# Experts' entry product: the last 64 features as three 64-row products on two row tiles

## The reference

```python
# layer 0: 8 experts of width 768, two of them weighted for each token
h_all = einsum('btc,che->bthe', x, w_fc)      # x: 520 tokens x 192 features
h = gelu(h_all of the token's experts)
o = sum over its experts of top_p * (h @ w_proj[expert])
# layer 1: 16 experts, eight of width 128 and eight of width 256, eight weighted for each token
for e in range(16):
    h = gelu(xt @ w1[:, off:off + wd])
    out = out + comb[:, e:e + 1] * (h @ w2[off:off + wd, :])
```

## Time and profile before

| what | value |
|---|---|
| median of 3 runs | 379.75 us (379.64 to 383.16) |
| the profiled execution's own time | 379.25 us |
| its span (first to last instruction of the program) | 377.4 us |
| granted clock of TensorE, mean | 0.857 |
| TensorE busy | 291.3 us of the span (77%) |
| VectorE busy | 268.6 us (71%) |
| ScalarE busy | 203.1 us (54%) |

### The profile page before, as it was taken

One profiled execution on the slowest core, in us unless ns is written; L12 is line 12 of the kernel. 1 busy time (PEld: TensorE's weight loads), 2 busy tenths in 40 slices (PEclk: granted clock), 3 DMA queues, 4 the chain that ended last, 5 costly groups with the idle time before them and its releaser, 6 DMA issues.

```text
span 377.4 us, 5949 instructions
## 1 busy us (share of the span) xinstructions
PE 291.3 (77%) x2232; PEld 266.6 (71%) x2232; DVE 268.6 (71%) x714; ACT 203.1 (54%) x486; POOL 23.6 (6%) x46
## 2 busy tenths in 40 slices
PE   5789979989999999999881042079631598999991
PEld 4577968889999999999771022058420588999991
DVE  1069173888888888798668997975368648888851
ACT  0034546677777777877271467570010667777750
POOL 8010000000000000000000005800000000000000
PEclk9999996999999999999996555569555579999997
DMA  7960400253153132000000000000500013543401
GB/s 235 261 267 1 148 0 4 85 176 125 50 177 116 61 146 72 29 1 2 0 3 0 0 1 2 0 0 2 195 0 1 0 24 114 162 160 126 113 0 43
DMA packets 11548, 27.36 MB, mean 72 GB/s; under 512 B 1496, under 2 KB 3144, under 8 KB 11520
## 3 DMA queue, kind: packets, MB, share of 16 engines
q1 hardware_dynamic: 10944, 26.03, 21.2%
q0 software_dynamic: 576, 0.96, 1.0%
HBM read 26.54 MB, written 0.45 MB: 72 GB/s over the span
## 4 chain that ended last, share of the span: by engine, by line
PE 62%; DVE 22%; ACT 7%; DMA 3%; issue 2%; SPq 2%; DVEq 0%; ACTq 0%
PE bank L585 26%; PE bank L647 9%; PE bank L569 7%; PE bank L632 4%; PE bank L630 4%; DMA embed_area<-w_tok_dram 3%; PE bank L847 2%; DVE embed_area L1510 1%; PE bank L552 1%; PE bank L832 1%; ACT hid_hi L982 1%; DVE bn L1187 1%; PE bank L844 1%; DVE stat_q L1395 1%; PE bank L857 1%
## 5 line engine op out<-in xcount | busy, mean ns | idle before, releaser
L585 PE MATMUL bank<-hid_hi,pj_parts 128*128 128x260 f32 x288 | 76.2, 286 | 1.7 <-DVE hid_lo L1282 1.7
L982 ACT ACTIVATE hid_hi<-hidden_area 128x260 fp32r<-128x260 f32 x144 | 55.9, 422 | 38.8 <-DVE hidden_area L1277 37.6
L1282 DVE TENSOR_TENSOR hid_lo<-hidden_area,hid_hi 128x260 fp32r<-128x260 f32 x144 | 56.6, 427 | 9.9 <-ACT hid_hi L982 0.3
L585 PEld LDWEIGHTS bank<-hid_hi,pj_parts 128*128 128x128 f32 x288 | 54.1, 188 | 2.5 <-DVE hid_lo L1282 2.0
L975 ACT ACTIVATE hidden_area<-bank 128x260 f32<-128x260 f32 x144 | 49.1, 377 | 6.9 <-PE bank L632 6.1
L585 PE MATMUL bank<-xt_hi,fc_hi 128*128 128x260 f32 x144 | 42.8, 297 | 1.3 <-ACT hidden_area L973 1.3
L632 PE MATMUL bank<-xt_lo,fc_lo 128*128 128x260 f32 x144 | 42.2, 293 | 0.0
L585 PE MATMUL bank<-xt_lo,fc_hi 128*128 128x260 f32 x144 | 41.5, 288 | 0.0
L630 PE MATMUL bank<-xt_lo,fc_hi 128*128 128x260 f32 x144 | 41.5, 288 | 0.0
L585 PE MATMUL bank<-xt_hi,fc_lo 128*128 128x260 f32 x144 | 41.3, 287 | 0.0
L647 PE MATMUL bank<-hid_hi,pj_parts 128*128 128x260 f32 x144 | 40.8, 283 | 0.0
(11 more groups left out here) (297 smaller groups left out, 559.3 us busy)
## 6 DMA issues: line engine op xcount, KB each, us to landing
raw_area<-fc_dram SPq DMA_DIRECT2D x8, 768.0 KB, 4.3
raw_area<-pj_dram SPq DMA_DIRECT2D x8, 576.0 KB, 5.4
xn<-comb_dram SPq DMA_DIRECT2D x12, 260.0 KB, 3.3
raw_area<-fc_dram SPq DMA_DIRECT2D x6, 512.0 KB, 4.0
hidden_area<-comb_dram SPq DMA_DIRECT2D x9, 260.0 KB, 3.3
raw_area<-pj_dram SPq DMA_DIRECT2D x6, 384.0 KB, 4.4
embed_area<-patches_dram SPq DMA_DIRECT2D x8, 256.0 KB, 4.7
embed_area<-w_tok_dram SPq DMA_DIRECT2D x8, 96.0 KB, 7.6
```

The source lines that it names most:

```text
L585: mm = pe.matmul(out, lhs[a], rhs[b], start=start and n == 0, stop=stop and n == 2, skip_group_check=True)
L982: act.activation(hid_hi[:, x % 3, tok], hid_w[:, x % 2, tok], ACT.Copy).then_inc(hid_hi_ready[y], 1)
L1282: dve.tensor_tensor(hid_lo[:, x % 3, tok], hid_w[:, x % 2, tok], hid_hi[:, x % 3, tok].bitcast(F32), ALU.subtract).then_inc(hid_lo_ready[y ...
```

## The change

The two 128-row matmuls with `x_mix` go. In their place come three products of 64 rows each (high x high, high x low, low x high), for the first half of the tokens on partitions 0 to 63 and for the second half on partitions 64 to 127, in turn. So `xt_hi[:, 1]` and `xt_lo[:, 1]` hold the first half's tokens on the lower and the second half's on the upper partitions, each made by two instructions of 64 x 260 in place of one of 64 x 520. The product low x low is no longer made. Per entry the array gets six matmuls of 64 rows where it had four of 128.

```diff
-        x_mix = xt_lo[:, 1, :]
...
                 pe.wait_ge(xhi_ready, 2 * n + (n + 1) // 2)
-                pe.wait_ge(xlo_ready, 2 * n)
+                pe.wait_ge(xlo_ready, 2 * n + (n + 1) // 2)
...
                             split3(out, (fc_hi[:, s, 0, cols], fc_lo[:, s, 0, cols]),
                                    (xt_hi[:, 0, tok], xt_lo[:, 0, tok]), True, False)
-
-                            pe.matmul(out, fc_hi[:, s, 1, cols], x_mix[:, tok], start=False, stop=False,
-                                      skip_group_check=True)
-                            mm = pe.matmul(out, fc_lo[:, s, 1, cols], x_mix[:, tok], start=False,
-                                           stop=True, skip_group_check=True)
-                        mm.then_inc(entry_mm[y], 1)
+                        if kind == "w":
+                            mm.then_inc(entry_mm[y], 1)
+                    if kind == "w":
+                        return
+                    for m, (f, v) in enumerate(((fc_hi, xt_hi), (fc_hi, xt_lo), (fc_lo, xt_hi))):
+                        for n in range(2):
+                            p, tok = slice(64 * n, 64 * n + 64), slice(n * HALF, (n + 1) * HALF)
+                            mm = pe.matmul(PB[PAIRS[k % 2][n]][:, 0:HALF], f[p, s, 1, cols], v[p, 1, tok], start=False,
+                                           stop=m == 2, skip_group_check=True)
+                            if m == 2:
+                                mm.then_inc(entry_mm[y], 1)
...
-                        k = DM // 2
-                        act.activation(xt_hi[k:DM, 1, :], xt[k:DM, 1, :], ACT.Copy).then_inc(xhi_ready, 1)
-                        act.activation(x_mix[0:k, :], xt[0:k, 1, :], ACT.Copy).then_inc(xhi_ready, 1)
+                        for n in range(2):
+                            q, tok = slice(64 * n, 64 * n + 64), slice(n * HALF, (n + 1) * HALF)
+                            act.activation(xt_hi[q, 1, tok], xt[q, 1, tok], ACT.Copy).then_inc(xhi_ready, 1)
```

More of the change, by code:

```diff
@@ L1220, in split_x @@
             def split_x(r):
[L1222 to L1225, removed]
+                every = slice(0, B * S)
+                parts = [(slice(0, chunk_rows(r)), 0, every)]
+                if r % 2:
+                    parts += [(slice(64 * n, 64 * n + 64), 1, slice(n * HALF, (n + 1) * HALF)) for n in range(2)]
+                else:
+                    parts += [(slice(0, DC), 1, every)]
+                for n, (p, j, tok) in enumerate(parts):
+                    dve.wait_ge(xhi_ready, 2 * (r - 1) + r // 2 + n + 1)
+                    dve.tensor_tensor(xt_lo[p, j, tok], xt[p, j, tok], xt_hi[p, j, tok].bitcast(F32),
                                       ALU.subtract).then_inc(xlo_ready, 1)
```

## The result

| | before | after |
|---|---|---|
| median | 379.69 us (4 runs) | **399.22 us** (4 runs, 397.2 to 406.94) |
| the profiled execution, its span | 379.25, 377.4 us | 400.2, 398.4 us |
| granted clock, mean | 0.857 | 0.842 |

The ratio is 1.051 (95% interval 1.045 to 1.056): slower by 5%, as forecast (396 us, 389 to 423). It leaves out the run of 406.94 us, a slow one, over 1.5% above the fastest of the same kernel.

What follows compares the result with a forecast made beforehand. PE alone was taken to bound the experts; 69 entries at + 0.266 us and three at + 0.38 made + 19.5 us, less 2.8 of waits, + 16.7 on 379.25: 396 us, range 389 to 423.

Steps and rivals of the forecast that it cites:

- What bounds the kernel: In both layers of experts PE alone bounds; what an entry takes more or less reaches the end 72 times.
- The pair, three slots for six: In each entry the six 64-row matmuls run side by side in three slots, 0.36 us; an entry gains 0.12 us.
- Rival 1: In the experts' entries the pairs don't overlap and take six slots in place of three: 422 us, chance 0.20.
- The change of tiling, 0.095 + 0.11 - 0.012: Before and behind an entry's pairs: stop plus unhidden weight load, less usual spacing; + 0.193 us each, + 0.386 an entry.
- Rivals 2 and 3: In the experts: a tiling change costs nothing, 371 us, chance 0.07; or the load stays hidden, 380 us, chance 0.09.
- Three entries at half clock, + 1.1 us: Entries 0 and 1 of layer 0 and 0 of layer 1 run at half clock, + 0.38 us each.
- The sum: Over the experts' entries: 69 at + 0.266 us and three at + 0.38 us, in all + 19.5 us before waits.
- The waits that hide a part, - 2.8 us: In the layers' first tiles PE's waits of 3.4 us for ACT and DVE shrink, hiding 2.8 us; bounds 0 and 3.4.
- What costs nothing: The split copies and subtraction on ACT and DVE, covered by the gate, and the later first-half result add no time.

Runs made afterwards that it cites:

- the run that has nothing else: The kernel before with only the last of an entry's ten matmuls using 64 rows in place of 128: 404.81 us, ratio 1.065.
- the repeat: The changed kernel run once more, unedited, for its spread and clock: 398.72 us, ratio 1.046.
- all in pairs: The changed kernel with all matmuls of the experts' entries and projections cut into pairs of 64 rows: 390.88 us, ratio 1.029.
- nine matmuls: The changed kernel with an entry's six 64-row matmuls replaced by three of 128 rows: 374.66 us; the kernel before without an entry's last matmul: 375.91 us.
- all in pairs, sooner: Same instructions as all in pairs, reordered on TensorE so more work lies between an entry and its projection: 384.31 us, ratio 1.008.

## Why the prediction was right, point by point

- **What bounds the kernel.** Right: TensorE in the experts, with every edit reaching the end tile for tile, as long as it made the tile longer. In the other direction the prediction didn't ask what is next; in layer 0 it is DVE with its work on the weights, which ends a load of six tiles at 14.24 us where TensorE took 14.5.
- **The pair, three slots for six.** Right. Column tiles had been the nearest row, and row tiles do the same: 0.12 us a pair, weight loads side by side, + 0.35 us an entry when the partner is taken away. Rival 1 is out. The Trainium skill, "TensorE: Matmul & The Clock Gate", section "Part 3: Packing small matmuls — row/col tiling", said so. The traces now agree for rows: the two starts of a pair are 0 to 6 ns apart in the changed kernel, mostly 2 to 4.
- **The change of tiling, 0.095 + 0.11 - 0.012.** Right: 0.20 and 0.19 us in the rows above against 0.193, and 25.1 us in the run that has nothing else, against 26.8. The stop that the gate showed for float32 and 8 columns, 0.095 us, was 0.09 us for float32r and 260 (0.209 from start to start, less 0.12). Rivals 2 and 3 are out. The drain that "TensorEngine Tiling (Array Packing)" of the Trainium skill names under "Key Properties" fits the stop of 0.1 us. The bare load, as large again, comes on top of it here.
- **Three entries at half clock, + 1.1 us.** Of the right kind, but the clock itself isn't fixed: it was 0.5 for 6.0 and 4.1 us of the layers before, for 9.1 and 5.3 after, for 6.1 and 10.2 in the repeat. The sum had no term for it: 4.3 us more at 0.5 are up to 2.1 us of time, in the repeat up to 3.1.
- **The waits that hide a part, - 2.8 us.** Too much: 1.0 us (3.4 to 2.4), in the repeat 1.7. The large ones stand (1.0 to 0.9 and 1.3 to 1.0 in the first run; in the repeat the second fell to 0.08, where layer 1 took 2.3 us more up to its first projection). The waits did hide the longer tile where they stood, and only there: from projection to projection the first three tiles of layer 0 took 2.87, 2.86 and 3.65 us before and 2.82, 2.86 and 3.65 after, the first of layer 1 3.96 both times. ScalarE and VectorE set the pace of these tiles; that it is their work on the weights was not tried for them. With 1.0 in its place the sum is 19.5 - 1.0 = 18.5, and 18.3 was measured. That fit is partly luck. The lower clock added up to 2.1 us that no term has. Against it the steady tile grew by 0.256 us and not by 0.266 (0.6 us for 58 tiles), since it was 2.413 and not 2.40 before, and the waits hid more than the 1.0 us that the view counts.
- **What costs nothing.** Right as far as the runs can tell: the stretch between the layers kept its 120.1 us with a split in it, and the order of halves made no difference (185.3 and 185.5 us). Ahead of the experts the length varies from 57.6 to 60.9 us among the traces without the dent, with the old split and with the new one, so an effect under 1 us can't be seen there.
- **396 for 399.** The term of the waits is 18.3 - 16.7 = 1.6 us of the miss. The rest is the dent in the clock: the profiled execution began the experts 2.9 us later, and the two executions with a higher mean clock took 398.2 and 397.2 us.

## What to carry to other kernels

In this kernel a matmul that used a smaller part of the array than its neighbours cost a stop and a bare weight load on the way in and again on the way out, 0.39 us together or 3.2 slots of 260 columns. That was so for one such matmul and for six. So count the changes of tiling first and the slots after. Fewer changes lost less: 399.2 us with all of them, 393.2 with about half, 390.9 and 384.3 with none. Yet none of these kernels was faster than the one before; with all in pairs the steady tile is shorter (2.28 us in layer 1 of the last kernel where 2.41 stood), but waits, the clock at the starts of the layers and their last tiles took it back. The price could be read before anything was built, at a place of the same kernel where the tiling changes already.

When the bound engine gets shorter by a slot, look at once for what is next: here about 3 us of the 8.6 that nine matmuls should gain went to the second engine. It stood under 2% behind (14.24 us a load against 14.5), which its busy share of 85% doesn't tell.

## What the runs showed of the hardware

- Row tiles of 64 rows run side by side in float32r with a weight load for each matmul: with all in pairs, sooner, 38 matmuls and 38 loads in 19 steps of 0.12 us, tile after tile (2.28 us a tile in the steady part of layer 1).
- The stop at a change of tiling was the same for float32 with 8 columns (0.095 us) and float32r with 260 (0.09 us); with the bare load a change costs 0.19 to 0.20 us at full clock. At half clock the stop is 0.35 - 0.22 = 0.13 us, as in bf16 there:

```profile
63.12 0.42 PE L583 MATMUL bank<-xt_hi,fc_lo 128*128 128x260 f32 x1
63.47 0.59 PE L634 MATMUL bank<-xt_hi,fc_hi 64*128 64x260 f32 x2
```

- The clock of one and the same program rises at another time from execution to execution (layer 1 of the changed kernel: 5.3 us and 10.2 us after its first entry), which is up to 2.5 us of time, as much as many a change is worth.
